# Mixture of experts: routing weights spread over the partitions by DMA from stored rows, in place of one matmul in each unit

## The reference, cut to what matters

```
logits = x @ router_w.T
probs = jax.nn.softmax(logits.astype(jnp.float32), axis=-1)
rw, sel = jax.lax.top_k(probs, K)
rw = rw / jnp.sum(rw, axis=-1, keepdims=True)

def body(acc, operand):
    e, wg, wu, wd = operand
    w_e = jnp.sum(jnp.where(sel == e, rw, jnp.zeros_like(rw)), axis=-1)
    h = jax.nn.silu(x @ wg) * (x @ wu)
    return (acc + h @ wd * w_e[:, None], None)
```

## Time and profile before

| what | before |
|---|---|
| time, median of 3 runs | 978.87 us (977.29 to 979.18) |
| span of the profiled execution | 976.2 us |
| PE busy | 874.2 us, 90% |
| PEld busy | 723.1 us, 74% |
| DVE busy | 720.7 us, 74% |
| ACT busy | 567.2 us, 58% |
| POOL busy | 305.8 us, 31% |
| DMA | 35.74 MB, mean 37 GB/s |
| units of the expert stage | from 469.4 to 683 us of the span |

### The profile page before, as it was taken

How to read it: one execution, slowest core, us unless ns; L and a number is a source line. 1 busy time by engine, 2 the same in 40 slices (tenths; PEclk the granted TensorE clock), 3 DMA queues, 4 the chain that set the end, 5 groups by cost and what they waited for, 6 DMA issues and landing times. The chain is left out here.

```text
span 976.2 us, 18548 instructions
## 1 busy us (share of the span) xinstructions
PE 874.2 (90%) x6894; PEld 723.1 (74%) x6896; DVE 720.7 (74%) x1207; ACT 567.2 (58%) x1714; POOL 305.8 (31%) x458
## 2 busy tenths in 40 slices
PE   1678999999999999978799999999899997999997
PEld 1667888888888888966577777777565554788886
DVE  7877989998999899788565444444788987566643
ACT  5667788778787778762453333333367775333432
POOL 1133434343333333341522222220323454042320
PEclk9989999999999999998899999999989998999999
DMA  4101010101010100003311111000100001010001
GB/s 154 44 1 66 2 66 2 66 1 66 2 66 1 66 2 23 2 2 134 123 51 52 52 52 51 3 0 0 65 1 2 2 1 51 21 60 33 32 0 44
DMA packets 10929, 35.74 MB, mean 37 GB/s; under 512 B 1248, under 2 KB 5344, under 8 KB 8544
## 3 DMA queue, kind: packets, MB, share of 16 engines
q1 hardware_dynamic: 10704, 34.64, 9.9%
q10 hardware_dynamic: 144, 0.03, 0.0%
HBM read 33.62 MB, written 1.05 MB: 36 GB/s over the span
## 5 line engine op out<-in xcount | busy, mean ns | idle before, releaser
L236 PE MATMUL ps<-wt_hi,xq 128*128 128x256 f32 (+1 forms) x512 | 123.7, 278 | 20.2 <-DVE ctx_lo L823 14.4
L236 PE MATMUL ps<-wt_lo,xq 128*128 128x256 f32 (+1 forms) x512 | 123.4, 282 | 0.0
L236 PEld LDWEIGHTS ps<-wt_hi,xq 128*128 128x128 f32 x512 | 99.7, 195 | 22.9 <-DVE ctx_lo L823 14.8
L413 ACT ACTIVATE square<-ps 128x128 bf16<-128x128 f32 x384 | 100.9, 295 | 26.0 <-PE ps L236 26.0
L236 PEld LDWEIGHTS ps<-wt_lo,xq 128*128 128x128 f32 x512 | 99.4, 194 | 0.0
L571 POOL TENSOR_TENSOR rstd<-rstd,half_neg 128x6 f32<-128x6 f32 x64 | 93.6, 1462 | 5.0
L1274 POOL TENSOR_TENSOR moe_w_lo<-moe_w_all,moe_w_hi 128x384 fp32r<-128x384 f32 x48 | 53.4, 1148 | 130.5 <-ACT moe_w_hi L1376 130.5
L1720 ACT ACTIVATE ca_probs<-ps 128x512 f32<-128x512 f32 x128 | 69.5, 594 | 31.1 <-PE ps L1636 30.2
L413 ACT ACTIVATION_READ_ACCUMULATOR square<-ps 128x1 f32 x384 | 85.9, 226 | 0.0
L1445 DVE TENSOR_TENSOR moe_act_g<-moe_act_g,ps 128x512 f32<-128x512 f32 x48 | 33.1, 689 | 67.2 <-PE ps L1311 67.2
L1392 ACT CAST moe_in_hi<-moe_inner 128x512 fp32r<-128x512 f32 x48 | 29.8, 620 | 89.1 <-DVE moe_inner L1448 77.6
(11 more groups left out here) (226 smaller groups left out, 2556.1 us busy)
## 6 DMA issues: line engine op xcount, KB each, us to landing
moe_w_all<-in_experts SPq DMA_DIRECT2D x8, 1152.0 KB, 5.1
w_in<-in_wt SPq DMA_DIRECT2D x8, 1024.0 KB, 5.8
wp_in<-in_wp SPq DMA_DIRECT2D x8, 512.0 KB, 3.6
ffn_codes<-in_codes SPq DMA_DIRECT2D x8, 384.0 KB, 3.1
ffn_w_scales<-in_code_scales SPq DMA_DIRECT2D x8, 384.0 KB, 3.8
x_rows<-in_x SPq DMA_DIRECT2D x2, 512.0 KB, 4.7
ctx_in<-in_ctxT SPq DMA_DIRECT2D x1, 1024.0 KB, 8.8
context_rows<-in_ctx SPq DMA_DIRECT2D x1, 1024.0 KB, 9.4
```

What stands on the lines that cost most here:

```text
L236: last = mm(ps[:, first + bank, col:col + width], left[:, c, tokens], w[:, c, wcol:wcol + width], start=(j == 0), stop=(j == len(steps) - 1))
L413: last = nc.scalar.activation(square[:, i % 2, j, :], ps[:, bank, (j % 4) * P:(j % 4) * P + P], ACT.Square, scale=float(HD) ** -0.5, accum ...
```

## The change

Ahead of the units nothing is different but one small DMA more (`merge`, 6 KB) and one pick matrix less. Behind the pick matmul of unit 0, PE adds the three parts of `rwT` up with two matmuls (`tensor_merge`, 32 x 512 each), so that float32 weight rows stand by expert; ACT copies them to `by_expert` (64 x 512), and SP stores them in DRAM as 32 rows of 4 KB (`stored_rows`) by two DMAs and waits for them to land. Units 0 to 5 (`j` = 0, `b` = 0) still use the pick matmul. For units 6 to 47 it is left out: SP reads for each block the row of each expert and writes it to all partitions of that expert, by two DMAs of 32, 64 or 96 partitions x 4 KB, 512 KB in all. They go to one of two buffers `shares` (128 x 1024 float32 each), and DVE's "inner" multiplies by that buffer instead of bank 2. A buffer is loaded again when "inner" of both units of the block before the last is done.

```
+            def load_shares(j, b, blk, free):
+                n = NBLK * b + blk
+                if free:
+                    sp.wait_ge(s["inner_done"], 2 * NBLK * 2 * j + 2 * n - 2)
...
+                    e = 4 * (2 * j + b) + expert
+                    sp.dma_start(shares[row:row + count, n % 2, :], router.stored_rows[bass.ds(e, 1), :].broadcast_to([count, TOKENS])
+                                 ).then_inc(s[f"shares_in{n % 2}"], 16)
...
-                if moe:
-                    if blk == 0 and half == 0:
-                        pe.wait_ge(s[f"pick_in{b}"], 16 * (j + 1))
+                if moe and picked(j, b):
                     if first:
+                        pe.wait_ge(s["pick_in"], 16)
                         router.tensor_turn(pe)
                         pe.wait_ge(router.rw_copied, 1)
                     else:
                         pe.wait_ge(s["inner_done"], v)
-                    mm(ps[:, R_BANK, :], pick[:, b, blk * P:blk * P + P], k.rwT[:, tokens], start=True, stop=True
+                    mm(ps[:, R_BANK, :], pick[:, blk * P:blk * P + P], k.rwT[:, tokens], start=True, stop=True
                        ).then_inc(s["r_ready"], 1)
+                    if first:
+                        router.tensor_merge(pe)
...
-                    dve.wait_ge(s["r_ready"], v + 1)
-                    nc.vector.tensor_tensor(inner[:, half, :], act_g[:, half, :], ps[:, R_BANK, :], ALU.mult).then_inc(s["inner_done"], 1)
+                    if picked(j, b):
+                        dve.wait_ge(s["r_ready"], v + 1)
+                        share = ps[:, R_BANK, :]
+                    else:
+
+                        n = NBLK * b + blk
+                        dve.wait_ge(s[f"shares_in{n % 2}"], 32 * (NBLK * j + n // 2 + 1 - (2 if n % 2 == 0 else 1)))
+                        share = shares[:, n % 2, half * 512:half * 512 + 512]
+                    nc.vector.tensor_tensor(inner[:, half, :], act_g[:, half, :], share, ALU.mult).then_inc(s["inner_done"], 1)
```

More of the change, by code:

```diff
@@ L997, in sync, with sync_store, tensor_merge, scalar_by_expert @@
         sp.dma_start(self.r_rows[:], self.a["router"]).then_inc(self.r_in, 16)
+        sp.dma_start(self.merge[:], self.a["merge"]).then_inc(self.merge_in, 16)
+    def sync_store(self, sp):
+        sp.wait_ge(self.by_expert_ready, 1)
+        for half in range(2):
+            sp.dma_start(self.stored_rows[:, 512 * half:512 * half + 512], self.by_expert[EXPERTS * half:EXPERTS * half + EXPERTS, :]
+                         ).then_inc(self.rows_stored, 16)
+        sp.wait_ge(self.rows_stored, 32)
+    def tensor_merge(self, pe):
+        E = EXPERTS
+        pe.wait_ge(self.merge_in, 16)
+        for half in range(2):
+            last = self.nc.tensor.matmul(self.k.ps[E * half:E * half + E, 3, :], self.merge[:], self.k.rwT[:, 512 * half:512 * half + 512],
+                                         start=True, stop=True)
+        last.then_inc(self.merged, 1)
+    def scalar_by_expert(self, act):
+        act.wait_ge(self.merged, 1)
+        self.nc.scalar.copy(self.by_expert[:], self.k.ps[0:2 * EXPERTS, 3, :]).then_inc(self.by_expert_ready, 1)
     def tensor_logits(self, pe):
@@ L1216, in gated_mlp @@
             w_lo = sb("w_lo", [P, 2, WALL], F32R)
-            pick = sb("pick", [3 * EXPERTS, 2, NBLK * P], BF16)
+            pick = sb("pick", [3 * EXPERTS, NBLK * P], BF16)
+            shares = sb("shares", [P, 2, TOKENS], F32)
         else:
@@ L1232, in gated_mlp, with picked @@
         used = "gated" if moe else "inner_done"
+        def picked(j, b):
+            return isinstance(j, int) and (j, b) == (0, 0)
         @block.sync
@@ L1241, in load @@
                     sp.dma_start(w_all[:, b, :], a["experts"][2 * j + b]).then_inc(s[f"w_in{b}"], 16)
-                    if free:
-                        sp.wait_ge(s["r_ready"], 2 * NBLK * (2 * j + b - 1))
-                    sp.dma_start(pick[:, b, :], a["pick"][2 * j + b]).then_inc(s[f"pick_in{b}"], 16)
                 else:
                     k.ffn.load(sp, j, b)
+            def load_shares(j, b, blk, free):
+                n = NBLK * b + blk
+                if free:
+                    sp.wait_ge(s["inner_done"], 2 * NBLK * 2 * j + 2 * n - 2)
+                row = 0
+                while row < P:
+                    expert, skip = divmod(P * blk + row, EXPERT_ROWS)
+                    count = min(EXPERT_ROWS - skip, P - row)
+                    e = 4 * (2 * j + b) + expert
+                    sp.dma_start(shares[row:row + count, n % 2, :], router.stored_rows[bass.ds(e, 1), :].broadcast_to([count, TOKENS])
+                                 ).then_inc(s[f"shares_in{n % 2}"], 16)
+                    row += count
             if moe:
@@ L1250, in _, with step @@
                 load(0, 0, False)
+                sp.dma_start(pick[:], a["pick"]).then_inc(s["pick_in"], 16)
                 load(0, 1, False)
                 k.context.sync(sp)
-            with sp.Fori(1, STEPS // 2) as j:
-                load(j, 0, True)
-                load(j, 1, True)
+                load(1, 0, True)
+                router.sync_store(sp)
+                load_shares(0, 1, 0, False)
+                load_shares(0, 1, 1, False)
+                load_shares(0, 1, 2, True)
+                def step(j, more):
+                    load(j, 1, True)
+                    for blk in range(NBLK):
+                        load_shares(j, 0, blk, True)
+                    if more:
+                        load(j + 1, 0, True)
+                    for blk in range(NBLK):
+                        load_shares(j, 1, blk, True)
+                with sp.Fori(1, STEPS // 2 - 1) as j:
+                    step(j, True)
+                step(STEPS // 2 - 1, False)
+            else:
+                with sp.Fori(1, STEPS // 2) as j:
+                    load(j, 0, True)
+                    load(j, 1, True)
             if not moe:
@@ L1405, in steps @@
                                 router.scalar_copy(act)
+                                router.scalar_by_expert(act)
                             if n == 1 and (moe or not first):
@@ L1946, in lay_out @@
     pick = np.tile(rows[None, :] == np.arange(EXPERTS)[:, None], (3, 1)).astype(mybir.dt.np(BF16))
-    arrays["pick"] = pick.reshape(3 * EXPERTS, STEPS, -1).transpose(1, 0, 2)
+    arrays["pick"] = pick.reshape(3 * EXPERTS, STEPS, -1)[:, 0]
+    arrays["merge"] = np.tile(np.eye(EXPERTS, dtype=np.float32), (3, 1)).astype(mybir.dt.np(BF16))
     by_step = lambda w: w.T.reshape(P, STEPS, P, 2).transpose(1, 0, 3, 2).reshape(STEPS, P, 2 * P)
```

8 lines of the change are left out of this document (7 added, 1 removed).

## The result

The changed kernel took 970.59 us (median of 4 runs, 964.96 to 974.83) beside 978.4 us for the kernel before on the same chip: a ratio of 0.9926, 95% interval 0.9897 to 0.9955, so 7.8 us faster. A second set, 7 runs, gave 968.0 us against 976.76 (26 runs of before): 0.9917 (0.9885 to 0.995).

A forecast was written before the change was run, and what follows sets the result against it. PE was taken to set the pace in nearly every expert unit. Picks -0.51 and -9.12, merge +0.35, slow pace +4.4 gave -4.9 us, so 974.0 us (969.6 at the fast pace); range 967.5 to 976.5.

The forecast's parts named there:

- fast pace kept: Rival: the experts' remaining matmuls stay at 0.2267 us each after the change, total 969.6 us; chance 0.36.
- What bounds the kernel: Expert stage: PE sets the pace in nearly every unit, so what leaves PE leaves the time.
- Picks: Units 6 to 47: picks 6 and 7 save 0.51 us, 11 to 46 save 9.12; 8 to 10 and 47 nothing.
- The merge: Two bf16 matmuls behind pick 0 add 0.35 us, between 0.25 side by side and 0.51 one after the other.
- The pace: From `down` of unit 9, 666 matmuls fall from 0.2267 to 0.2333 us each, losing 4.4 us; chance 0.47.
- more than that: Rival: the last stage too runs at the fast pace, 3.8 us more gained, total 965.8 us; chance 0.04.
- DVE's "inner": Reading two SBUF operands instead of one from PSUM adds up to 0.07 us a unit, inside 1.03 us of slack: nothing.
- DMAs: Share loads of 512 KB a block land in time, even behind a weight load, and don't slow PE: nothing.
- late shares: Rival: share transfers take over 8.4 us a block, so DVE and PE wait; about 1197 us; chance 0.07.
- eaten up: Rival: new waits in every unit or SBUF writes slowing PE's reads cancel the gain; about 978 us; chance 0.06.
- The start: SP's extra 6 KB ahead of the first weights costs one issue, hidden before ACT copies these weights.

The follow-up runs named there:

- `pick_kept`: Changed kernel with the old pick matmul put back into units 6 to 47, its output unread; 977.4 us, ratio to before 1.0011.
- `no_spread`: Kernel before without the pick matmuls of units 6 to 47 and nothing in their place, no shares by DMA, no merge; 969.74 us.
- `pool_sixth`: Changed kernel with Pool taking one piece of the weights' low parts instead of six, from the third weight set on; 964.25 us in one run.
- `combined`: Changed kernel with DVE's context subtractions halved, behind units 4, 6, 10 and 11, and 736 unused bytes ahead of the last stage's tiles; 960.59 us, ratio to before 0.9841.
- `last_stage_bf16`: Changed kernel with a bf16 matmul of 512 columns put behind U in eight units of the last stage; 971.53 us.

## Why the prediction was right, and where not

The time lay in the range, and the side was right: 974.0 forecast, 970.59 measured. But the likeliest case was the wrong one: what came is the rival "fast pace kept", 969.6. The range held both cases, so the time alone speaks for neither; that it fell inside in spite of the wrong choice is luck, and the gain was 7.8 and 8.8 us where 4.9 had been forecast.

**What bounds the kernel.** Right, and shown: with the slots back in PE's row the gain is nil (`pick_kept`), with nothing but the slots taken it is 9.33 us (`no_spread`).

**Picks.** I counted 9.63 in units 6 to 47; 9.33 came. Picks 11 to 46 are right: from the last U of unit 11 to that of unit 47 it is 156.0 us before and 146.88 in `no_spread`, 9.12 less. The missing 0.3 lies between the last U of unit 7 and that of unit 11, 17.51 us before and 17.56 in `no_spread`, where my sum had 0.25 less. Picks 8 to 10 brought nothing, as said, because of the chain on DVE. But the wait it leaves appears at two places (0.61 and 0.88 in `no_spread`), and after each the first two matmuls start about 0.34 apart instead of 0.23. The sum had one wait of 0.8 us and no restart; the restarts alone are 0.2 us.

**The merge.** 0.54 us, past both my value (0.35) and its upper end (0.51), and not because the two run one after the other: they start together. What I left out is their neighbours. Before, the first large matmul started 0.04 us behind pick 0; now the pair starts 0.32 behind it, and the large matmul another 0.32 later.

**The pace: the step that failed.** "After the change PE comes to `down` of unit 9 behind a wait ..., with no pick behind it to reset it", and so, I took, at the slow pace for 666 matmuls, +4.4 us. The waits came (1.02 and 0.88 on the weight load), and the pace stayed. I had read two paces in two stages and made of them a state that a pick resets. The picks were the difference I looked for, not the only one there was: the tiles' places differ too, and moving them moves the pace in both directions (0.2267 to 0.2333 for G and U of the experts, 0.2333 to 0.2267 in the last stage), while adding a pick-like matmul does not. The rival "more than that" (the last stage fast as well) fell: 135.34 us after the change, as before.

**DVE's "inner".** Forecast: nothing, "up to 0.07 us a unit". Wrong in its mechanism. Six of the 42 took 1.30 to 1.42 us, beside Pool. Five hide in the slack I counted (1.03 us; 0.27 of it is left there); the one behind unit 8 stands in the chain without slack. The second column is 0.54 us longer than in `no_spread` (173.16 less 172.62): 0.46 between the last U of unit 7 and that of unit 11 (18.02 less 17.56), and 0.08 spread over the units behind, where PE has no wait; what that rest is stays open. A row of before had warned: the context subtraction of the earlier trace rows took 2.98 us while Pool was at work, and its twin behind unit 4 2.29:

```profile
495.23 2.29 DVE L971 TENSOR_TENSOR context_split<-context_rows,context_split 64x2048 fp32r<-64x2048 f32 x1
```

The Trainium skill, "SBUF — State Buffer", section "SBUF: two separate sides", has the rule that I left out: DVE with two SBUF inputs and a Pool operation that reads SBUF share a pair of ports under an exclusive lock, and the later of the two waits for the whole instruction. The rows agree: 0.69 us became 1.42 at most, and the 0.73 added is less than one piece of Pool (1.02); and with one operand in PSUM, 0.69.

**DMAs.** Nothing, as forecast. 14 x 384 KB in 3.6 us and 14 x 256 KB in 3.9 us at the median, no wait for them anywhere; `pool_sixth` and `combined`, with all of this traffic, run the units at 171.6 us, which is 42 x 18 matmuls at 0.2267 (171.4), the slot of pick 5, and no more. So the rivals "late shares" and "eaten up" fell. The Trainium skill, "DMA: Bandwidth & Descriptors", section "Rules for kernel authors", confines a leading broadcast of c copies, with c under 16, to at most c engines; with 32 to 96 copies the landings show no sign of that, 384 KB in 3.6 us beside a plain 512 KB in the same time.

**The start.** SP's extra 6 KB ahead of the first weights: hidden in all profiles but the first, where ACT waited 0.71 us for these weights (and 0.04 in one more). Whether the 6 KB made them late there isn't shown.

In sum: -9.33 for the slots, +0.54 for the merge, +0.54 for the long "inner" and the rest beside it: -8.25 us, against medians that fell by 7.8 and 8.8. By my own sum the fast pace would have given -9.3.

## What to carry to other kernels

On an engine that never waits, an instruction taken out is worth its pitch in that row, wherever no chain on another engine is as long as the row; count such a chain from its start to its end, and add a restart for each wait that it causes. Moving an operand from PSUM to SBUF is not neutral where another engine works in SBUF at the same time: look for long ones among like instructions before calling it free. And where two stages run the same instruction at two speeds, list all that differs between them, the addresses of tiles too, before one difference is made the cause.

## What the runs showed of the hardware

- **The place of the tiles, most likely of the streamed rows, sets the pace of fp32r matmuls** of 128 x 512 at the full clock: 0.2267 us with turned rows that start at a multiple of 1024 bytes in a partition, 0.2333 at 32 or 288 bytes behind one, 0.2288 at 320, 0.2323 at 384. The inner's parts ran at 0.227 at 512 bytes behind (`no_spread`) and at 768 (the changed kernel), and at 0.2315 at 832. All the fast places are multiples of 256 and none of the slower ones is; no run was made to test that, and why the slower ones differ stays open.
- **DVE and Pool delay each other** where both take all operands from SBUF: DVE's 0.69 us became up to 1.42, its 1.22 became 1.92 and its 2.29 became 2.99; Pool's 1.02 became 1.47. With a PSUM operand, 43 of 43 on DVE took 0.69 (`no_spread`).
- **Spreading a stored row over partitions by DMA** (up to 384 KB out of one row of 4 KB) lands in 2.3 to 5.5 us.
- **A bf16 matmul put into a row of fp32r ones** costs 0.22 us in the last stage (`last_stage_bf16`) and 0.253 among the experts (`no_spread` against before).
